# The fronts of a relative-position attention: where queries are expanded, who spills keys and values, how many filler matmuls run

## The reference, cut to what matters

```python
q = hidden_states @ Wq.T + bq
k = hidden_states @ Wk.T + bk
v = hidden_states @ Wv.T + bv
score_1 = jnp.einsum('bhqd,bhkd->bhqk', q_head, k_head)
rpk = _rel_table_lookup(rel_k, T, T)
q_resh = q_head.reshape(B * H, T, D).transpose(1, 0, 2)
score_2 = jnp.einsum('qmd,qkd->qmk', q_resh, rpk)
...
attn = jax.nn.softmax((score_1 + score_2) / scaling, axis=-1)
weight_1 = jnp.einsum('bhqk,bhkd->bhqd', attn, v_head)
```

## Time and profile before

| | |
|---|---|
| Median of 3 runs | 1613.85 us (1613.04 to 1617.98) |
| Span of the profiled execution | 1612.7 us |
| PE busy in that span | 1383.0 us, 86% |
| DVE busy | 1018.2 us, 63% |
| ACT busy | 758.2 us, 47% |
| Front of stage D, with the wait for the first scores | about 376 to 426.4 us from the start |

### The profile page before, as it was taken

One profiled execution on the slowest core, in us unless ns is written; L12 is line 12 of the kernel. 1 busy time (PEld: TensorE's weight loads), 2 busy tenths in 40 slices (PEclk: granted clock), 3 DMA queues, 4 the chain that ended last, 5 costly groups with the idle time before them and its releaser, 6 DMA issues.

```text
span 1612.7 us, 44300 instructions
## 1 busy us (share of the span) xinstructions
PE 1383.0 (86%) x17837; PEld 862.6 (53%) x17837; DVE 1018.2 (63%) x2607; ACT 758.2 (47%) x1942; POOL 236.9 (15%) x216
## 2 busy tenths in 40 slices
PE   5889898696499999998966989898989898899755
PEld 4343443483267676766743457445654565357545
DVE  4467666324477777776744777667767776777633
ACT  1313133251266566665632367245734474437534
POOL 2011220123030030020001110012000200030035
PEclk8989999798699999999997999899998999899968
DMA  9600000023230010100014000000000000000031
GB/s 323 248 16 1 16 3 6 22 59 97 77 145 4 24 23 10 37 3 17 4 25 101 1 1 2 3 14 1 2 3 14 1 2 1 2 13 1 1 92 51
DMA packets 56617, 59.09 MB, mean 37 GB/s; under 512 B 27853, under 2 KB 42064, under 8 KB 55264
## 3 DMA queue, kind: packets, MB, share of 16 engines
q1 hardware_dynamic: 53600, 50.97, 9.9%
q0 software_dynamic: 2528, 5.27, 1.0%
q10 hardware_dynamic: 288, 0.03, 0.0%
HBM read 32.56 MB, written 24.14 MB: 35 GB/s over the span
## 4 chain that ended last, share of the span: by engine, by line
PE 72%; DVE 14%; issue 4%; SPq 3%; DMA 3%; ACT 2%; POOL 2%; ACTq 0%; POOLq 0%; DVEq 0%
PE ps L1167 8%; PE ps L1555 6%; PE ps L265 6%; PE ps L1574 5%; PE ps L1147 5%; PE ps L1588 4%; PE ps L1157 4%; PE ps L1188 4%; DVE arena L612 4%; PE ps L1543 3%; PE ps L486 3%; PE ps L1202 2%; PE ps L1597 2%; PE ps L510 2%; DVE arena L1693 1%
## 5 line engine op out<-in xcount | busy, mean ns | idle before, releaser
L1300 DVE TENSOR_REDUCE nmax<-ps 128x1 f32<-128x512 f32 x256 | 166.8, 683 | 60.6 <-PE ps L1157 60.0
L1630 ACT ACTIVATE arena<-ps,arena 128x512 f32<-128x512 f32 (+3 forms) x256 | 135.3, 531 | 115.9 <-DVE arena L1693 110.0
L1693 DVE TENSOR_REDUCE arena<-ps 128x1 f32<-128x512 f32 (+3 forms) x256 | 124.4, 487 | 72.8 <-PE ps L1559 70.8
L1260 ACT ACTIVATE arena<-ps,nmax 128x512 f32<-128x512 f32 x172 | 118.8, 691 | 84.1 <-DVE nmax L1300 83.0
L1574 PE MATMUL ps<-sqc,arena 128*128 128x128 f32 x640 | 107.4, 290 | 20.3 <-DVE arena L1701 20.2
L1308 DVE COPY arena<-ps 128x512 f32<-128x512 f32 x128 | 88.0, 688 | 36.8 <-PE ps L1167 35.3
L612 DVE TENSOR_REDUCE arena<-ps 128x8 f32<-128x1232 f32 x64 | 89.1, 1438 | 32.6 <-PE ps L474 32.5
L265 PE MATMUL ps<-identb 128*128 128x512 bf16 x366 | 108.5, 462 | 1.4 <-DVE kcol L746 1.4
L1701 DVE TENSOR_SCALAR arena<-arena 128x512 f32<-128x512 f32 (+3 forms) x256 | 100.8, 394 | 9.1
L1555 PE MATMUL ps<-arena 64*128 64x384 f32 (+3 forms) x512 | 105.1, 489 | 0.0
L1588 PE MATMUL ps<-arena 128*64 128x128 f32 x1280 | 97.3, 282 | 0.0
(11 more groups left out here) (355 smaller groups left out, 2628.1 us busy)
## 6 DMA issues: line engine op xcount, KB each, us to landing
xs_d<-onehot SPq DMA_DIRECT2D x4, 2560.0 KB, 27.0
cw<-in_cw SPq DMA_DIRECT2D x2, 2048.0 KB, 10.9
rv<-in_rv SPq DMA_DIRECT2D x2, 1536.0 KB, 17.1
late<-in_gw SPq DMA_DIRECT2D x3, 1024.0 KB, 11.1
arena<-gs_d SPq DMA_DIRECT2D x23, 129.0 KB, 2.1
onehot<-q_s SPq DMA_DIRECT2D x96, 8.0 KB
arena<-xs_d SPq DMA_DIRECT2D x23, 64.0 KB, 1.8
xs_d<-arena SPq DMA_DIRECT2D x23, 64.0 KB, 1.6
```

What stands on the lines that cost most here:

```text
L1260: nc.scalar.activation(PB[k % 6], ps[:, k % 5, :], ACT.Exp, bias=nmax[:, u:u + 1], accum_out=rsum[:, b % 2, u:u + 1]).then_inc(SD["exp"], 1)
L1300: nc.vector.tensor_reduce(nmax[:, k % NU:k % NU + 1], ps[:, k % 5, :], AX.X, ALU.max, negate=True)\
L1630: nc.scalar.activation(TF["p%d" % (n % 2)][:, h * S:h * S + wd], ps[:, FSB[n % 2][h], 0:wd], ACT.Exp, bias=TF["nmax"][:, k4:k4 + 1], accum ...
L1693: nc.vector.tensor_reduce(TF["nmax"][:, k4:k4 + 1], ps[:, FSB[n % 2][h], 0:wd], AX.X, ALU.max, negate=True)\
```

## The change

Four edits:

1. The stores of keys, values and x leave SP's queue. ACT issues the store of keys right behind the move that makes them (with a semaphore `kst` of its own), and the stores of values and x of batch b - 1 in `act_D0_spill`, behind the transposed copy and the square root of the norm that ACT does for the next batches. `spill` now counts 32 for each batch.
2. SP, having stored the queries of a batch, waits only for that store and issues the eight read-backs. The loads `QO` and `KT` move from behind batch 0 to behind batch 1's read-backs; the load of values of batch 0 (`VT[0]`) moves behind the last spill.
3. DVE builds the first tables (`build_own`, `build_first`) behind all four batches instead of between batches 1, 2 and 3.
4. The filler matmuls of stage D are 4 instead of 14 for batches 1 to 3.

```diff
-            for _ in range(0 if k == "G" and b + 1 < B else FILL[k][0]):
+            for _ in range(0 if k == "G" and b + 1 < B else 4 if k == "D" and b else FILL[k][0]):
...
             act_transpose(act, b, "D")
             if b + 1 < B:
                 act_root(act, b + 1, "D")
+            if b:
+                act_D0_spill(act, b - 1)
             kb = COLB.index("D_bk")
             act.wait_ge(SD["kp"], b * 3 + 2)
             if b:
-                act.wait_ge(SD["spill"], b * 48)
+                act.wait_ge(SD["kst"], b * 16)
             nc.scalar.activation(TD0["kt"], ps[:, 2 + 3 * (b % 2), :], ACT.Identity, bias=colb[:, kb:kb + 1]).then_inc(SD["kt"], 1)
+            act.wait_ge(SD["kt"], b + 1)
+            nc.scalar.dma_start(one_s(k_s, b), TD0["kt"]).then_inc(SD["kst"], 16)
+
+        def act_D0_spill(act, b):
+
+            act.wait_ge(SD["v"], b + 1)
+            nc.scalar.dma_start(one_s(v_s, b), TD0["v"]).then_inc(SD["spill"], 16)
+            nc.scalar.dma_start(one_s(x_s, b), own_x(b).rearrange("p i n -> p (i n)")).then_inc(SD["spill"], 16)
...
             dve.wait_ge(SD["kp"], b * 3 + 3)
             if b:
-                dve.wait_ge(SD["spill"], b * 48)
+                dve.wait_ge(SD["spill"], b * 32)
...
+        def sp_D0(sp, b):
+            sp.wait_ge(SD["qt"], b * 2 + 2)
+            sp.dma_start(one_s(q_s, b), q_t[:, :]).then_inc(SD["qsp"], 16)
+            sp.wait_ge(SD["qsp"], 16 * b + 16)
+            sp_D_other(sp, 0, b, (0, 1) if b + 1 < B else (0,))
             if b == 1:
-                build_own(dve, nc.vector, 0)
-            if b == 2:
-                build_first(dve, 0)
-
-        def sp_D0(sp, b):
-            one = lambda a, b: a[b:b + 1].rearrange("o p n -> p (o n)")
-            sp.wait_ge(SD["qt"], b * 2 + 2)
-            sp.dma_start(one(q_s, b), q_t[:, :]).then_inc(SD["qsp"], 16)
+                sp.dma_start(QO, one_s(q_s, 0)).then_inc(SD["ldk"], 16)
+                sp.wait_ge(SD["kst"], 16)
+                sp.dma_start(KT[0], one_s(k_s, 0)).then_inc(SD["ldk"], 16)
             if b + 1 == B:
-                sp.wait_ge(SD["qsp"], 16 * B)
-                sp_D_other(sp, 0, b, (0,))
-            sp.dma_start(one(x_s, b), own_x(b).rearrange("p i n -> p (i n)")).then_inc(SD["spill"], 16)
-            sp.wait_ge(SD["kt"], b + 1)
-            sp.dma_start(one(k_s, b), TD0["kt"]).then_inc(SD["spill"], 16)
-            sp.wait_ge(SD["v"], b + 1)
-            if b + 1 == B:
-                sp.dma_start(VT[0], one(v_s, 0)).then_inc(SD["ldv"], 16)
-            sp.dma_start(one(v_s, b), TD0["v"]).then_inc(SD["spill"], 16)
-            sp.wait_ge(SD["spill"], b * 48 + 48)
-            if b + 1 < B:
-                sp.wait_ge(SD["qsp"], 16 * b + 16)
-                sp_D_other(sp, 0, b, (0, 1))
-            if b == 0:
-                sp.dma_start(QO, one(q_s, 0)).then_inc(SD["ldk"], 16)
-                sp.dma_start(KT[0], one(k_s, 0)).then_inc(SD["ldk"], 16)
+                sp.wait_ge(SD["spill"], 32 * B)
+                sp.dma_start(VT[0], one_s(v_s, 0)).then_inc(SD["ldv"], 16)
...
             act.wait_ge(SD["qsp"], 16 * B)
             sp_D_other(nc.scalar, 0, B - 1, (1,))
+            act_D0_spill(act, B - 1)
...
             dve.wait_ge(s_prep, 7)
             nc.vector.tensor_reduce(rvcol[:, 0:1], rvd, AX.X, ALU.add).then_inc(s_prep, 1)
+            build_own(dve, nc.vector, 0)
+            build_first(dve, 0)
             dve_D(dve)
```

More of the change, by code:

```diff
@@ L966, in decoder @@
         SDq = [sem("s_d_ldq%d" % i) for i in range(2)]
-        SD = {n: sem("s_d_" + n) for n in ("qsp", "ldk", "ldv", "kp", "kt", "qt", "v", "spill", "ld", "a", "rk", "rv", "sc", "max", "exp", "t", "pta",
+        SD = {n: sem("s_d_" + n) for n in ("qsp", "kst", "ldk", "ldv", "kp", "kt", "qt", "v", "spill", "ld", "a", "rk", "rv", "sc", "max", "exp", "t", "pta",
                                            "ptv", "pv", "oex", "sum", "rin", "ee", "r", "yn", "y2", "yst", "ao", "at")}
@@ L1032, in act_D0, with one_s @@
             if b:
-                act.wait_ge(SD["spill"], b * 48)
+                act.wait_ge(SD["kst"], b * 16)
             nc.scalar.activation(TD0["kt"], ps[:, 2 + 3 * (b % 2), :], ACT.Identity, bias=colb[:, kb:kb + 1]).then_inc(SD["kt"], 1)
+            act.wait_ge(SD["kt"], b + 1)
[4 more added lines that the diff above has]
+            nc.scalar.dma_start(one_s(x_s, b), own_x(b).rearrange("p i n -> p (i n)")).then_inc(SD["spill"], 16)
+        def one_s(a, b):
+            return a[b:b + 1].rearrange("o p n -> p (o n)")
         def by_unit(a, z):
@@ L1268, in copy @@
                 if Q == 0:
-                    act.wait_ge(SD["spill"], 48 * B)
+                    act.wait_ge(SD["spill"], 32 * B)
+                    act.wait_ge(SD["kst"], 16 * B)
                 nc.scalar.copy(PT[:, Q % 2, j, :], ps[:, TB[0], :]).then_inc(SD["pta"], 1)
@@ L1356, in dve_D @@
                 top(k)
-            dve.wait_ge(SD["spill"], 48 * B)
+            dve.wait_ge(SD["spill"], 32 * B)
+            dve.wait_ge(SD["kst"], 16 * B)
             for Q in range(NQ):
@@ L2098, in _ @@
             load_ctx(0, 1)
+            sp.wait_ge(SD["kst"], 16 * B)
+            sp.wait_ge(SD["spill"], 32 * B)
             sp_D_load(sp, 1)
```

## The result

The changed kernel takes 1600.12 us (median of 4 runs, 1597.92 to 1601.1), the kernel before 1614.01 in the same comparison: a ratio of 0.991, 95% interval 0.9889 to 0.9931, 13.9 us less. The forecast was 1606.0 and a range from 1602.5 to 1609.5, so the direction was right and the size was not.

The account below looks back on a forecast made before the run. The prediction took SP's loop of query stores, landings and read-backs to bound stage D's front; its terms summed to 35.36 us against 43.24, 7.9 less, so 1613.85 - 7.9 = 1606.0 us, range 1602.5 to 1609.5.

Parts of the forecast that it names:

- The bound of the front: Front of stage D: a loop through SP of query store, landing, eight read-backs and next store sets the pace.
- rival A: Front of stage D: SP's loop as summed, 7.9 us less (6.5 to 9); chance 0.58.
- B: Front: store 2 lands quickly because spills are spread in time; up to 10.9 us less, 1603.0; chance 0.16.
- The sum of the front: From the store of batch 0's queries to PE's first scores: 35.36 us against 43.24, 7.9 us less.
- The stores of queries: SP's queue in the front: stores near 390.4, 398.7 and 408.7, before 395.05, 407.62 and 416.60.
- The waits of DVE, ACT and PE inside the loop: Front: queries ready 1.8, 2.3 and 4.1 us ahead of SP, moved tables 3.3 us ahead; all covered.
- PE's clock: Front, between batches: may fall to half clock with fewer fillers; queries 1 delayed 0.95 us, inside 1.8, costing nothing.
- Rival E: Main part: clock returns later after a longer PE wait, about 12.7 us more work at half clock; slower, 1618.7; chance 0.04.
- Rival D: Front: spills crowd stores, so stores 1 and 3 also take 5.1 us; 2.0 us less in all, 1611.9; chance 0.08.
- the one on the main part: Stage D behind the front, 426.4 to 800 us: PE-bound, can't absorb or add much, so front gains reach the end in full.
- worth some 0.3 us at most: Front, PE ahead of queries 1: ten fewer fillers there gain this little; the other 20 lie where PE waits anyway.

Follow-up runs that it names:

- the five kernels of the first row of the table: Changed kernel, kernel before with 4 fillers, and three changed kernels with other queues; no matmuls added to the changed kernel's count; main parts 415.16, 415.69, 414.78, 414.08, 415.00 us.
- 98 pads in the kernel before: Kernel before plus 98 unread matmuls of 16 columns between batch 3's projections and the first scores, where PE waits; 1606.58 us, ratio 0.9961.

## Why the prediction was wrong, point by point

**The bound of the front** was named rightly: SP's loop. Tables alone gave nothing, spills and fillers most, and taking the loads out of the loop gave 2.1 us where 2.3 was expected. The front's 8.8 us lie in rival A's range (6.5 to 9); the 13.9 of the whole lie beyond every rival, B's 10.9 included.

**The sum of the front** was 35.36 us and is 34.42. The terms that were off: the first store landed in 3.0 instead of 2.2, its read-backs took 5.42 instead of 5.08, and store 2 landed in 3.48, where the sum took 5.1 of the earlier trace rows. The bounds of 2.1 and 5.1 held it. From the last store's landing to `build_second` it was 4.70 instead of 5.14. Store 1 landed in 2.2, as taken. The first two make the front longer and the others shorter, so part of the sum's nearness is luck.

**The stores of queries** came at 8.48, 16.60 and 25.07 behind the first, where the sum gives 7.3, 15.6 and 25.6.

**The waits of DVE, ACT and PE inside the loop** were covered, as said. The waits that the prediction named, in the changed kernel's timeline:

```profile
393.51 0.69 DVE L1077 TENSOR_TENSOR arena<-ps,rowb 128x512 f32<-128x512 f32 x1 [1.13 <-DMA x_s<-late]
...
407.34 0.87 DVE L1071 TENSOR_SCALAR q_t<-ps,colb 128x256 f32<-128x256 f32 x2 [7.45 <-DMA q_s<-q_t]
...
409.86 3.65 DVE L1396 TENSOR_TENSOR arena<-x,m 128x1024 f32<-128x1024 f32 x2
...
419.07 2.36 DVE L1402 TENSOR_TENSOR cw<-rv,m 128x1024 f32<-128x1024 f32 x2 [3.30 <-DMA rv<-q_s]
```

Values 1 wait 1.13 us for the spill, queries 3 wait 7.45 for store 2, and `build_second` still waits 3.30 behind the two moved tables, where the prediction had 3.3 as their cover.

**PE's clock.** In the changed kernel it didn't fall between batches 1 and 3; even batch 3's queries, made at half clock before (2.07 us), now take 1.13. The rows of batches 1 and 3:

```profile
389.07 1.13 PE L1017 MATMUL ps<-xnT,sqw 128*128 128x512 f32 x2 [0.68 <-ACT xnT L277]
...
398.90 1.13 PE L1017 MATMUL ps<-xnT,sqw 128*128 128x512 f32 x2 [0.72 <-ACT xnT L277]
```

That isn't so in every kernel with 4 fillers: with half of the read-backs on ACT the clock fell for batch 2, as told above. Rival E didn't come: the clock stood at 1.2 GHz for the first 12.0 us of the main part (421.6 to 433.6) against 10.6 before, 1.4 us more, where E needed 12.7.

**Rival D**, spills that crowd the stores: stores 1 and 3 landed in 2.2 and 2.1, so no. The Trainium skill, "DMA: Bandwidth & Descriptors", section "Issuing engines are not separate DMA queues", allows another issuer to save issue time alone. The trace agrees that issue time is saved, and shows one thing besides: with the stores went SP's waits for their landing, 4.14 us at the first of them, which stood between its issues.

**The step that failed** is the one on the main part: "what the front gains, the end gains, microsecond for microsecond". I took fillers for time alone, "worth some 0.3 us at most" (they are worth 1.7 in the front), and gave no thought to what 60 instructions fewer do to everything behind them in PE's stream. The runs put in its place a term of 6.8 us. That is the mean of the main parts with 30 added matmuls without the kernel before (421.57) less the mean with none (414.74, the five kernels of the first row of the table and the one with 98 in the kernel before). The profile of the kernel before, with 424.18, lay 2.6 above its like, so the 9.0 between the first two profiles is probably too much; with it in the mean the term would be 7.5. With 8.8 for the front this makes 15.6, inside the measured interval (11.1 to 17.9 us). The same 6.8 explains the comparisons of the experiments within theirs, for example 98 pads in the kernel before, 6.6 by the sum and 6.3 measured; 4 fillers in the kernel before, 9.0 and 7.9.

What is shown: the length of the main part depends on the number of PE instructions ahead of it and not on their time, and comes back after 256 more, one packet's worth (one period was tried). The stall followed above moves through the program with that number, matmul for matmul, and every such stall ends shortly behind the start of a packet of queue 8. That PE stalls because the next packet hasn't come follows from this, though no view names the packet as the releaser. What sets when a packet starts stays open; at the longest stall, with 96 pads, the DMA engines were busy all the time (share 1.00 from 450 to 454 us), but no run takes those transfers away. Open too are the stretches ahead and behind: the first store of queries came between 381.5 and 387.4 us from the start, and the rest took 757.5 to 763.8 us, without a relation to the edits that I can see.

## What to carry to other kernels

When a queue stores something, waits for it to land and reads it back, lay out that queue's own loop, issue times and landings, before costing anything else; a transfer moved to an engine that idles is worth its issue time and the wait behind it, and an edit that moves compute out of the way is worth nothing until that loop is shorter. When an edit adds or removes instructions ahead of a long dense PE stage, cut the executions at marks and compare the stage itself, and try a few counts of harmless matmuls in an idle stretch ahead of it: here they moved the main part by up to 8 us and took no time where they stood. A gain of under 1% measured with such an edit must not be credited to the idea behind it until a pad has given the position back.

## What the runs showed of the hardware

- The main part of stage D, about 20,770 PE instructions (matmuls and weight loads), took 415.2, 419.3, 422.0, 423.6, 420.5 and 415.3 us with 0, 15, 30, 64, 96 and 128 small matmuls added ahead of it.
- A stall of PE in it moved by as many matmuls as were added (behind 35, 20 and 5 of one group with 0, 15 and 30), and all 93 stalls of the main parts of 14 traces ended 2.2 to 3.0 us behind the start of a packet of queue 8.
- Ninety-eight matmuls added to the kernel before made it 6.3 us faster (ratio 0.9961).
- ACT issued stores of 256 KB in 0.33 to 0.48 us each, and four read-backs of 8 KB, strided pieces, took it 3.43 us, where SP needs 2.45.
- In the changed kernel the granted clock stayed at 2.4 GHz from batch 1 to batch 3 with 4 fillers for each; with half of the read-backs on ACT, behind a wait of 2.72 us, batch 2's queries were made at 1.2 GHz (1.98 us instead of 1.13).
- Between 440 and 810 us the clock fell to 1.2 GHz in two kernels of 14, behind stalls of 2.02 and 3.50 us.
